# The third layer norm's normalising pass on ScalarE instead of VectorE, in a two-layer graph and expert network

## The reference, cut to what matters

```
x  = x + L0_ffn(layernorm(x))     # mixture of 8 experts, each node goes to 2 of them
xn = layernorm(x)                 # the third layer norm: (x - m) / sqrt(v + 1e-5)
h  = relu(xn @ Wd + bd) @ Wu + bu + xn     # low-rank adapter of the graph layer
h  = relu(gcn(h, W1, b1));  h = gcn(h, W2, b2)
x  = x + h + L1_mix(xn)           # L1_mix begins with a layer norm of xn
```

## Time and profile before

| | us |
|---|---|
| median of 3 runs | 2983.23 (2977.67 to 2984.29) |
| profiled execution | 2981.63 |
| its span in the profile | 2979.9 |
| TensorE busy | 2729.0 (92%) |
| VectorE busy | 1482.0 (50%) |
| ScalarE busy | 965.4 (32%) |
| chain that ended last: TensorE | 80% |
| chain that ended last: VectorE | 11% |

### The profile page before, as it was taken

How to read it: one execution, slowest core, us unless ns; L and a number is a source line. 1 busy time by engine, 2 the same in 40 slices (tenths; PEclk the granted TensorE clock), 3 DMA queues, 4 the chain that set the end, 5 groups by cost and what they waited for, 6 DMA issues and landing times.

```text
span 2979.9 us, 31067 instructions
## 1 busy us (share of the span) xinstructions
PE 2729.0 (92%) x11881; PEld 1889.5 (63%) x11881; DVE 1482.0 (50%) x2251; ACT 965.4 (32%) x1579; POOL 126.2 (4%) x146
## 2 busy tenths in 40 slices
PE   6998649999989899989985999999799999899999
PEld 5785335678986556667863865556577777455555
DVE  7994549979993364431116120133476776322220
ACT  7893100068871142212211202022344443322210
POOL 1000030000000001100012000000000000000000
PEclk9999969999999899969996999999899999899999
DMA  9800341021103301179965320000201100300000
GB/s 243 301 0 1 105 113 60 27 85 51 50 4 68 72 23 32 54 245 360 358 237 144 68 67 17 16 1 15 71 29 35 36 29 16 116 6 11 11 11 11
DMA packets 131740, 238.13 MB, mean 80 GB/s; under 512 B 18639, under 2 KB 99572, under 8 KB 131118
## 3 DMA queue, kind: packets, MB, share of 16 engines
q1 hardware_dynamic: 116418, 192.97, 21.2%
q0 software_dynamic: 15200, 43.44, 4.4%
HBM read 173.10 MB, written 63.25 MB: 79 GB/s over the span
## 4 chain that ended last, share of the span: by engine, by line
PE 80%; DVE 11%; DMA 4%; issue 2%; ACT 2%; POOL 1%; DVEq 1%; SPq 0%; ACTq 0%; POOLq 0%
PE ps L930 22%; PE ps L1322 14%; PE ps L1306 14%; PE ps L884 5%; PE ps L1130 4%; PE ps L1179 4%; PE ps L1190 4%; PE ps L947 3%; DVE arena L1890 3%; DVE arena L1891 2%; PE ps L1243 1%; DMA spill_w<-arena 1%; PE ps L1040 1%; PE ps L1232 1%; DMA arena<-in_x_dram 1%
## 5 line engine op out<-in xcount | busy, mean ns | idle before, releaser
L930 PE MATMUL ps<-arena 128*125 128x384 f32 x2160 | 716.7, 492 | 10.3 <-issue 5.9
L930 PEld LDWEIGHTS ps<-arena 128*125 128x125 f32 x2160 | 407.4, 190 | 296.5 <-issue 22.5
L1322 PE MATMUL ps<-arena 128*125 128x384 f32 x1280 | 416.1, 489 | 14.4 <-DVE arena L2273 14.4
L1306 PE MATMUL ps<-arena 128*128 128x312 f32 (+1 forms) x1536 | 407.1, 427 | 15.0 <-DVE arena L2273 15.0
L1306 PEld LDWEIGHTS ps<-arena 128*128 128x128 f32 x1536 | 292.1, 190 | 129.8 <-issue 16.8
L1322 PEld LDWEIGHTS ps<-arena 128*125 128x125 f32 x1280 | 241.7, 189 | 188.7 <-issue 17.6
L1334 ACT ACTIVATE arena<-ps 128x750 f32<-128x750 f32 (+5 forms) x140 | 109.1, 780 | 669.6 <-PE ps L930 208.5
L2273 DVE SCALAR_TENSOR_TENSOR arena<-arena 128x1250 f32<-128x1250 f32 (+1 forms) x170 | 231.4, 1383 | 114.3 <-PE ps L1306 110.8
L884 PE MATMUL ps<-arena 128*125 128x380 bf16 x1280 | 212.5, 327 | 9.9 <-DVE arena L1722 9.9
L1826 DVE SCALAR_TENSOR_TENSOR arena<-ps,arena 125x768 f32<-125x768 f32 x30 | 28.7, 956 | 355.3 <-PE ps L1322 293.5
L884 PEld LDWEIGHTS ps<-arena 128*125 128x125 bf16 x1280 | 172.7, 137 | 49.5 <-DVE arena L1722 12.6
(11 more groups left out here) (309 smaller groups left out, 2664.5 us busy)
## 6 DMA issues: line engine op xcount, KB each, us to landing
arena<-in_L_ffn_W_dram SPq DMA_DIRECT2D x54, 1152.0 KB, 8.1
xs_rows<-arena SPq DMA_DIRECT2D x1, 30720.0 KB, 99.6
arena<-in_kw_dram SPq DMA_DIRECT2D x24, 512.0 KB, 4.7
arena<-al_dst POOLq DMA_DIRECT2D x18, 625.0 KB, 4.8
arena<-xs_rows SPq DMA_DIRECT2D x27, 384.0 KB, 7.7
y_rows<-arena POOLq DMA_DIRECT2D x27, 384.0 KB, 6.7
arena<-in_kw_dram SPq DMA_DIRECT2D x6, 1536.0 KB, 10.1
arena<-in_x_dram SPq DMA_DIRECT2D x2, 3600.0 KB
```

The source lines that it names most:

```text
L930: mm = pe.matmul(slot(g)[0:TILE, 512 * half:512 * half + HALF], xt[:, k, i * TILE:i * TILE + TILE], w[:, k, :], start=(k == 0), stop=(k == ...
L1306: mm = pe.matmul(slot(g)[:, 512 * b:512 * b + wd_], w[:, r % 2, ORDER[p], o * P:o * P + P], feat[place(f)][:, lo + b * wd_:lo + b * wd_ + ...
L1322: mm = pe.matmul(slot(g)[0:TILE, 512 * b:512 * b + HALF], fv[:, q, :], w2c[m][q][:, b * HALF:b * HALF + HALF], start=(p == 0 and q == 0), ...
```

## The change

The program that makes the third layer norm is rewritten. VectorE no longer makes the 125x768 pass. In its place (`lowered`) it makes the reciprocal and one 125x1 operation, `nmean` = -mean x inverse deviation, and raises `ev("shifted")`. ScalarE makes the pass (`normalised`): it takes the root, waits for `ev("shifted")`, and writes `H` as `acc` times inverse deviation plus `nmean`, both taken from a column; that raises `ev("ln_x3")`. In ScalarE's queue the root and the pass of tile i + 1 now stand ahead of the copy-out of tile i, and so also ahead of `low_rank(0)` for i = 6. `nmean` gets ten columns of its own. TensorE's, GpSimd's and SyncE's programs are as before.

```diff
@@ -427,6 +427,9 @@
+        nmean = rcut(NT)[0:TILE]
+        assert ro[0] <= 4700
@@ -1539,8 +1542,16 @@
-            for i in range(NT):
+            def normalised(i):
                 root_of(i)
+                act.wait_ge(ev("shifted"), i + 1)
+                act.activation(H[:, i, :], acc[:, i, :], ACT.Identity, bias=nmean[:, i:i + 1], scale=rstd[:, i:i + 1])\
+                   .then_inc(ev("ln_x3"), 1)
+
+            normalised(0)
+            for i in range(NT):
+                if i + 1 < NT:
+                    normalised(i + 1)
                 turned_tile("x3", i, xT)
                 if i == 6:
                     act.wait_ge(ev("u_ones"), 1)
@@ -2183,6 +2194,12 @@
+            def lowered(i, n):
+                dve.wait_ge(ev("std"), n)
+                chain(dve.reciprocal(rstd[:, i:i + 1], stdv[:, i:i + 1]))
+                dve.scalar_tensor_tensor(out=nmean[:, i:i + 1], in0=mv[:, i, 0:1], scalar=-1.0, in1=rstd[:, i:i + 1],
+                                         op0=ALU.mult, op1=ALU.mult).then_inc(ev("shifted"), 1)
+
@@ -2201,8 +2218,8 @@
                 counted.append(statistics(t, acc))
                 if t >= 1:
-                    normal("x3", t - 1, counted[t - 1], acc, H)
-            normal("x3", NT - 1, counted[NT - 1], acc, H)
+                    lowered(t - 1, counted[t - 1])
+            lowered(NT - 1, counted[NT - 1])
```

More of the change, by code:

```diff
@@ L1540, in low_rank @@
                       ACT.Relu, bias=bd_c[0:RANK])
+            def normalised(i):
+                root_of(i)
+                act.wait_ge(ev("shifted"), i + 1)
+                act.activation(H[:, i, :], acc[:, i, :], ACT.Identity, bias=nmean[:, i:i + 1], scale=rstd[:, i:i + 1])\
+                   .then_inc(ev("ln_x3"), 1)
+            normalised(0)
             for i in range(NT):
-                root_of(i)
+                if i + 1 < NT:
+                    normalised(i + 1)
                 turned_tile("x3", i, xT)
```

## The result

| | before | after |
|---|---|---|
| median | 2981.07 us (2977.41 to 2984.29, 11 runs) | 2971.72 us (2969.22 to 2976.65, 11 runs) |
| ratio | | 0.9973, 95% interval 0.9963 to 0.9982 |
| profiled execution, its span | 2981.63, 2979.9 | 2969.87, 2968.1 |

The change makes the kernel faster by 0.27%, 8 us by the ratio (5 to 11 us by its interval) and 9.35 us by the medians. The forecast was 2975.1 us and a gain of 8.1.

What follows compares the result with a forecast made beforehand. VectorE's tile loop, then the order of ScalarE's queue, were taken to bound the start of `down(1)`. 3.1 + 5.0 = 8.1 us off 2983.2 gave 2975.1 us, eight-in-ten range 2970.5 to 2980.2.

Steps and rivals of the forecast that it cites:

- What bounds: Third layer norm: VectorE's loop, then an order of queues, set the start of `down(1)`, which moves 8.1 us earlier.
- The period: VectorE's loop over the ten token tiles: 4.25 us a tile becomes 3.72, or 3.84 by the upper bound.
- The pass: The 125x768 pass on ScalarE takes 0.835 + 0.09 = 0.93 us; it was 0.68 on VectorE.
- After `down(0)`: ReLU pass to end of pass 9: 4.4 us in place of 9.44; VectorE's wait some 4 us long.
- The split into 3.1 and 5.0: Start of `down(1)`: 3.1 us from the shorter period up to `down(0)`, 5.0 from the new order behind it.
- The clock: TensorE between `down(0)` and `down(1)`: clock expected to fall again in a 7 us gap; late rises cost 1.3 and 1.6 us.
- A: The whole sum holds with TensorE's clock as before: gain 8.1 us; chance 0.70.
- case C: TensorE's clock rises later in both projections, or the gather falls behind: gain 5.2 us, time 2978.0; chance 0.14.
- The reload: SyncE's reload of the matrix still lands before the multiplication that needs it, with a margin of at least 1.6 us.
- the gather: The gathered rows reach VectorE's adds in time: 3 us in hand at tile 9, about 1 for the middle tiles.
- D: ScalarE loads a table, 1.283 us, at every change between pass and root: time 2986; chance 0.05.
- The time: Whole kernel: 2983.2, from the median of three runs, less 8.1 gives 2975.1 us.

Runs made afterwards that it cites:

- bias_only: The changed kernel with the pass taking only its bias from a column, without the multiplication by the inverse deviation; single time 2973.07 us.
- order_only: The kernel before with only ScalarE's queue reordered, root of tile i + 1 ahead of copy-out of tile i; VectorE keeps its pass; 2971.6 us, ratio 0.9967.
- move_only: The changed kernel with each tile's root and pass put back behind the copy-out of the tile before; 2980.03 us, ratio 1.0002.
- filler: The changed kernel with TensorE turning tiles 7 and 8 twice, to fill its gap before `down(1)`; 2970.2 us, ratio 0.996.

## Why the prediction was right

- **What bounds.** Right: the stage was VectorE's loop and then an order of queues, and the start of `down(1)` moved by 8.2 us, 8.1 forecast.
- **The period.** 3.73 measured, 3.72 forecast. The small operation cost 0.08 where the lower bound, 0.07, was taken.
- **The pass.** Under-sized: 1.03 us where 0.93 was taken. The step that failed is the price of the operands: one from a column was added where the instruction has two. bias_only measured 0.935 with one. It cost 0.1 us at each of three places. The estimate by the Trainium skill, "ScalarE: Activation LUTs", section What ACT_TABLE_LOAD costs, 1.01 us, was the nearer one to the 1.03 measured.
- **After `down(0)`.** 4.54 us from the ReLU pass to the end of pass 9, 4.4 forecast; VectorE's wait was 4.05, some 4 forecast.
- **The split into 3.1 and 5.0.** As terms of one sum they were right, but they are not the worth of the move and of the order. The order alone gave all the time that was gained (order_only, ratio 0.9967), the move alone none (move_only, 1.0002). The 5.0 holds two effects that the prediction didn't tell apart: 7.5 us from the order, and 2.3 that are lost again with the last two passes on ScalarE. So most of the 3.1 us of the period is paid back behind `down(0)`.
- **The clock.** It fell in the gap, as forecast for A, and rose later than in the profile before: `down(1)` took 8.88 us, so 0.85 of the 8.2 went back. That was in the range by case C's mechanism. The prediction took the start of `down(1)` for what counts; the end moved by 7.3. What it lacked is that the same gain was to be had without the fall.
- **The reload.** Issued at 1603.90, and L1246 at 1650.07 didn't wait for it. Beyond the first tile, where it waits in every version, VectorE did not wait for the gather in the changed kernel's profile. No ACT_TABLE_LOAD lay between root and pass, so D is out.
- **The time.** 2971.72 against 2975.1. Of the 3.4 us, 2.2 are the basis: the three runs had their median at 2983.23, eleven have it at 2981.07. The other 1.2 are scatter as far as the record shows: the profiles account for 7.3 us, the medians differ by 9.35, and an interval from 5 to 11 us can't tell these apart. That the ratio gives 8 where 8.1 was forecast is partly luck.

## What to carry to other kernels

Before work is moved from a busy engine to an idle one, look at which instruction the busy engine waits for longest in that stage, and what stands ahead of that instruction in its queue. Here a 125x1 root stood behind a pass that waited for a 7.7 us projection; taking it ahead was worth as much alone as with the move, and freeing VectorE without it only lengthened VectorE's wait. Once the order is right, the rest is balance. Here it helped the schedule to give the last passes to VectorE, which had nothing left to do (`down(1)` starts at 42.1 in place of 43.45), though in time that step is within the scatter.

## What was not expected of the hardware

Most of the scatter between executions of one kernel goes with TensorE's clock: in the first eleven runs of the changed kernel, the two with a mean granted clock of 0.954 took 2976.52 and 2976.65 us, and the three with 0.958 took 2969.87, 2971.72 and 2971.81. Which of the two causes the other isn't shown by these figures. But within the stage a gain in the schedule can be gone by where the clock falls: `down(1)` takes 6.48 us at 2.4 GHz and took 8.88 in the changed kernel. And more work in the gap did not keep the clock: filler lost it with TensorE busy for 3.28 us of the 5.04 before the fall.
